# Four block boundaries of a one-core decoder kernel: which queue issues which load and store, and when

## The reference, cut to what matters

```python
x = x + tanh(g_xattn[0]) * L0_xattn(layernorm(x), ctx, ctx)      # 8 heads of 8, softmax over 256
x = x + tanh(g_ffn[0])   * L0_ffn(layernorm(x), ...)
x = x + tanh(g_xattn[1]) * L1_xattn(layernorm(x), ctx, ctx)      # q and k scaled to length 1 in each head
...
def L0_ffn(x, router_weight, router_bias, gate_up_proj, gate_up_bias, down_proj, down_bias):
    logits = x @ router_weight.T + router_bias                    # 16 experts
    top_val, top_idx = top_k(logits, 4); top_val = softmax(top_val)
    gate_up = einsum('th,ehd->etd', x, gate_up_proj) + gate_up_bias[:, None]   # 256 -> 512
    gate, up = min(gate_up[..., ::2], 7), clip(gate_up[..., 1::2], -7, 7)
    out = einsum('etd,edh->eth', (up + 1) * gate * sigmoid(1.702 * gate), down_proj) + down_bias[:, None]
    return sum over the token's 4 experts of score * out
```

## Time and profile before

| | |
|---|---|
| time, median of 3 runs | 3649.17 us (3646.26 to 3651.99) |
| the profiled execution: time / span of its instructions | 3641.4 us / 3639.7 us |
| PE busy / weight loads (PEld) | 2865.4 us (79%) / 1830.7 us (50%) |
| DVE / ACT / POOL busy | 2155.6 us (59%) / 1480.0 us (41%) / 1110.8 us (31%) |
| DMA | 386.10 MB, mean 106 GB/s |
| mean granted TensorE clock | 0.887 of 2.4 GHz |
| stretches, from the timeline: front; attention 0 | 0 to 144; 144 to 573 us |
| norms, router and ranks; scatter beside keys and values | 575 to 690; 691 to 926 us |
| experts 0; combine and split; attention 1 begins | 926 to 1421; 1426 to 1574; 1578 us |

### The profile page before, as it was taken

The page is one execution under the profiler, slowest core; times in us unless marked ns, Lnnn a source line. Parts: engine busy times, 40 slices in busy tenths (PEclk is TensorE's granted clock), DMA queues, the critical chain, the costliest instruction groups (busy, mean ns, idle before and its releaser), DMA issues. The chain is left out here.

```text
span 3639.7 us, 60306 instructions
## 1 busy us (share of the span) xinstructions
PE 2865.4 (79%) x20178; PEld 1830.7 (50%) x20178; DVE 2155.6 (59%) x4946; ACT 1480.0 (41%) x3032; POOL 1110.8 (31%) x1494
## 2 busy tenths in 40 slices
PE   5488884466699995579947798999989749999993
PEld 4233333222355553433323486454568638888782
DVE  7699993577577776634468687888868620000003
ACT  5377772155222223579935454222245211112120
POOL 3211110277233335512279542000034441111110
PEclk7599996599899998579968899999989669999996
DMA  7766643299422224858500341000044221112204
GB/s 255 204 117 119 119 103 139 91 366 363 166 81 81 79 82 123 201 97 118 101 1 1 123 150 56 1 1 1 1 141 143 92 63 57 50 54 65 72 28 139
DMA packets 261609, 386.10 MB, mean 106 GB/s; under 512 B 56865, under 2 KB 188942, under 8 KB 261056
## 3 DMA queue, kind: packets, MB, share of 16 engines
q1 hardware_dynamic: 236160, 314.07, 32.3%
q0 software_dynamic: 25152, 68.22, 5.4%
HBM read 227.49 MB, written 160.24 MB: 107 GB/s over the span
## 5 line engine op out<-in xcount | busy, mean ns | idle before, releaser
L3167 POOL DMA_INDIRECT rows_out<-e_out,e_tr_dest x224 | 235.5, 1051 | 870.8 <-DVE e_out L3804 504.4
L3804 DVE COPY e_out<-e_psD 128x512 f32<-128x512 f32 x40 | 27.7, 692 | 492.3 <-PE e_psD L3772 492.1
L1237 ACT ACTIVATE a_pt<-a_psS 128x512 f32<-128x512 f32 x512 | 277.6, 594 | 102.0 <-PE a_psS L1133 97.7
L1259 DVE TENSOR_REDUCE a_mx_sb<-a_psM 128x4 f32<-128x1024 f32 x256 | 293.2, 1213 | 9.2 <-PE a_psM L1116 8.2
L3572 PE MATMUL e_psG<-e_wgu,e_yT 128*128 x576 | 275.1, 600 | 25.9 <-ACT e_yT L3600 23.3
L1147 PE MATMUL a_psV<-a_pt,a_vt 128*18 128x256 f32 x4096 | 291.1, 386 | 1.2 <-issue 0.8
L3772 PE MATMUL e_psD<-e_w,e_hT 128*128 128x256 f32 x1280 | 289.9, 386 | 0.0
L3761 PE MATMUL e_psH<-e_yT,e_w 128*128 128x256 f32 x1280 | 284.9, 381 | 1.6 <-issue 0.8
L3704 ACT ACTIVATE e_hT<-e_psH 128x512 f32<-128x512 f32 x160 | 95.6, 597 | 452.6 <-PE e_psH L3761 452.6
L3761 PEld LDWEIGHTS e_psH<-e_yT,e_w 128*128 128x128 f32 x1280 | 244.4, 191 | 35.7 <-issue 2.1
L3772 PEld LDWEIGHTS e_psD<-e_w,e_hT 128*128 128x128 f32 x1280 | 245.5, 194 | 33.3
(11 more groups left out here) (433 smaller groups left out, 6221.1 us busy)
## 6 DMA issues: line engine op xcount, KB each, us to landing
kbd<-e_bgu SPq DMA_DIRECT2D x64, 512.0 KB, 4.6
cr_kbd<-kbd SPq DMA_DIRECT2D x64, 512.0 KB, 3.4
rows_in<-zeros POOLq DMA_DIRECT2D x36, 522.0 KB, 6.3
e_xin<-rows_in SPq DMA_DIRECT2D x144, 128.0 KB
vbd<-e_bd SPq DMA_DIRECT2D x64, 272.0 KB, 4.0
cr_vbd<-vbd SPq DMA_DIRECT2D x64, 272.0 KB, 2.6
cq_rows<-rows_out SPq DMA_DIRECT2D x32, 512.0 KB, 12.1
e_w<-in_L_ffn_w_dram SPq DMA_DIRECT2D x16, 1024.0 KB, 7.6
```

The costliest lines, as they stand in the source:

```text
L1237: act.activation(pt[:, probs(t, h), b, :, :], psS[:, unit(t, h, b) % S_BANKS, :].rearrange("p (k c) -> p k c", k=KC), ACT.Exp, scale=scale ...
L1259: dve.tensor_reduce(mx[:, t % 2, :, h, :], psM[:, k % 2, :, :].rearrange("p b (f c) -> p b f c", f=2), AX_X, ALU.max).then_inc(ring_read, 1)
L3167: pool.indirect_dma_start(out=self.rows_out[0:limit, :], out_offset=bass.IndirectOffsetOnAxis(ap=self.dest[:, t:t + 1], axis=0), in_=rows, ...
```

## The change

1. Front: slot 0 is loaded one group earlier (SP, end of group 2). SP keeps only the third piece's store of the last group; ACT issues the other two and the four `turned` stores at the end of its list. Slot 1 is loaded by SP at the start of the attention (`early` is 1, two slots stay allocated), followed by the values of tiles 0 and 1, the first shift, the next values and slot 2.
2. Layer 0's experts (`class Experts0`): the first matrices and their bias (`load_up`, 17 DMAs) are issued in `phase_project` behind the router's rows and bias. The second matrices (4 DMAs of 1024 KB) and their bias are issued by ACT in `phase_experts0` (`load_down`), behind its first copy of turned rows. `KeysValues` uses the room of the second matrices and second bias instead. PE waits for the second matrices before the first L3589, DVE for the bias before the first L3648. SP fetches the rows of tiles 0 and 1 ahead of the destinations.
3. Combine: slots 0 and 1 are loaded in steps 6 and 7, q and k together; slots 2 and 3 at the start of layer 1's attention.

```diff
@@ phase_front, sync @@
-                    if g == NG - 1:
+                    if g < NG - 1:
+                        for piece, n_done in enumerate((n_hi, n_mid, n_lo)):
+                            sp.wait_ge(n_done, g + 1)
+                            store_normal(sp, g, piece)
+                    if g == NG - 2:
                         for operand in ("q", "k"):
                             slots.load(sp, operand, 0)
-                    for piece, n_done in ((0, n_hi), (1, n_mid), (2, n_lo)):
-                        sp.wait_ge(n_done, g + 1)
-                        sp.dma_start(n_pieces[...], np[:, piece, :, :] ...).then_inc(n_stored, 16)
-                for m, (_, dst) in enumerate(pairs):
-                    sp.wait_ge(w_copied, m + 1)
-                    sp.dma_start(dst..., wt[:, m, :, :]).then_inc(w_stored, 16)
-                for operand in ("q", "k"):
-                    slots.load(sp, operand, 1)
+                sp.wait_ge(n_lo, NG)
+                store_normal(sp, NG - 1, 2)
                 sp.wait_ge(ct_stored, 16 * NG)
@@ phase_front, scalar @@
                 normal_mid(NG - 1)
+                act.wait_ge(n_hi, NG)
+                store_normal(act, NG - 1, 0)
+                act.wait_ge(n_mid, NG)
+                store_normal(act, NG - 1, 1)
+                act.wait_ge(w_copied, n_w)
+                for m, (_, dst) in enumerate(pairs):
+                    act.dma_start(dst..., wt[:, m, :, :]).then_inc(w_stored, 16)
@@ phase_attend, sync @@
+                for s in range(slots.early, 2):
+                    slots.load(sp, "q", s)
+                    slots.load(sp, "k", s)
                 load_values(0)
-                load_values(1)
-                if slots.early < BUFS:
-                    slots.load(sp, "q", 2)
                 if with_max:
                     shift(0)
-                if slots.early < BUFS:
+                load_values(1)
+                slots.load(sp, "q", 2)
+                if with_max:
                     sp.wait_ge(ones_set, 1)
-                    slots.load(sp, "k", 2)
+                slots.load(sp, "k", 2)
@@ phase_project, sync (phase_norms has no prefetch any more) @@
                     sp.dma_start(b[:, :], bias...).then_inc(bias_loaded, 16)
+                if prefetch is not None:
+                    prefetch(sp)
@@ phase_scatter, sync @@
                     pairs.sync(sp)
-                    late(sp)
@@ phase_combine_split, sync @@
-                    if i < slots.early:
-                        slots.load(sp, "k", i)
-                    if i in (4, 5):
-                        sp.wait_ge(stored[i % 2], 16 * PIECES)
-                        for s in range(2 * i - 8, 2 * i - 6):
-                            slots.load(sp, "q", s)
+                    if i == 4:
+                        sp.wait_ge(stored[0], 16 * PIECES)
+                    if 0 <= i - 6 < slots.early:
+                        slots.load(sp, "q", i - 6)
+                        slots.load(sp, "k", i - 6)
@@ expert_weights0 and expert_biases0 become class Experts0 @@
+    def load_up(self, sp):
+        for e in range(self.E):
+            sp.dma_start(self.wgu[:, e, :, :], self.gate_up[e]...).then_inc(self.up_loaded, 16)
+        sp.dma_start(self.bgu[:, :, :], self.gate_up_b...broadcast_to([P, self.E, self.D2])).then_inc(self.up_loaded, 16)
+
+    def load_down(self, eng):
+        n = self.E // self.PARTS
+        for m in range(self.PARTS):
+            eng.dma_start(self.wd[:, m * n:(m + 1) * n, :, :],
+                          self.down[m * n:(m + 1) * n]...).then_inc(self.down_loaded, 16)
+        eng.dma_start(self.bd[:, :, :], self.down_b...broadcast_to([P, self.E, self.D])).then_inc(self.bias_loaded, 16)
@@ phase_experts0 @@
+                    sp.dma_start(xin[:, t % 2, :], rows_in[t, :, 0:DIM]).then_inc(fetched[t % 2], 16)
+                    if t == 1:
+                        token_rows.load(sp, rows_in, 0)
+                    if t >= 1:
                         token_rows.load(sp, rows_in, t)
...
-                pe.wait_ge(loaded, 16 * (2 * E + 2))
+                pe.wait_ge(weights.up_loaded, 16 * (E + 1))
...
                         pe.wait_ge(h_copied, t + 1)
+                        if t == 0:
+                            pe.wait_ge(weights.down_loaded, 16 * weights.PARTS)
...
                     t, u = s + 2, s % 2
+                    if t == 1:
+                        weights.load_down(act)
...
                         dve.wait_ge(down_done, t + 1)
+                        if t == 0:
+                            dve.wait_ge(weights.bias_loaded, 16)
@@ flamingo_decoder @@
-            slots = Slots(core, c, "a0", q_pieces, k_pieces, 2)
+            slots = Slots(core, c, "a0", q_pieces, k_pieces, 1)
-            slots = Slots(core, held, "a1", q_pieces, n_pieces, Slots.BUFS)
+            slots = Slots(core, held, "a1", q_pieces, n_pieces, 2)
```

More of the change, by code:

```diff
@@ L174, in group, with store_normal @@
             return slice(g * G, (g + 1) * G)
+        def store_normal(eng, g, piece):
+            eng.dma_start(n_pieces[g, :, :, PIECES - 1 - piece].rearrange("b h d t c -> (b h) d (t c)"),
+                          np[:, piece, :, :].rearrange("p t c -> p (t c)")).then_inc(n_stored, 16)
         with nc.Block() as block:
@@ L250, in _ @@
                                    pattern=[[HD, H]], channel_multiplier=-1).then_inc(sel_made, 1)
-                for m in range(slots.early):
+                for m in range(slots.held_first):
                     pool.memset(slots.of("k", m), 1.0).then_inc(ones_set, 1)
@@ L442, in phase_norms @@
         with nc.Block() as block:
-            if prefetch is not None:
-                @block.sync
-                def _(sp):
-                    prefetch(sp)
             @block.vector
@@ L919, in __init__ @@
         self.loaded = [core.lasting_sem(f"{name}_ql{m}") for m in range(self.BUFS)]
-        self.hold(ctx, "first", range(early), "right")
+        self.hold(ctx, "first", range(held_first), "right")
     def hold(self, ctx, part, slots, side=None):
@@ L969, in phase_attend @@
         pt = core.sb(ctx, n + "_pt", [P, EXP_BUFS, 2, KC, DIM], F32)
[L970 to L971 removed]
+        slots.hold(ctx, "rest", range(slots.held_first, BUFS))
         ctl = core.sb(ctx, n + "_ctl", [P, 2, 2, 2 * KC, 2, 4, HD], F32)
@@ L1016, in _ @@
                 if with_max:
-                    for m in range(slots.early, BUFS):
+                    for m in range(2, BUFS):
                         pool.memset(slots.of("k", m), 1.0).then_inc(ones_set, 1)
@@ L2791, in _, with phase_scatter @@
                 c.link(dve.tensor_copy(slot[:, :, :], pos[:, :, :]))
-def phase_scatter(core, name, K, slot, rows_in, limit, mark, prefetch, pairs=None, late=None):
+def phase_scatter(core, name, K, slot, rows_in, limit, mark, prefetch, pairs=None):
     nc = core.nc
@@ L3616, in _ @@
                 expert = experts(mybir.EngineType.DVE)
-                dve.wait_ge(loaded, 16 * (2 * E + 2))
+                dve.wait_ge(weights.up_loaded, 16 * (E + 1))
                 for s in range(-1, T0 + 2):
```

83 lines of the change are left out of this document (39 added, 44 removed).

## The result

The changed kernel takes 3610.12 us (median, 3607.72 to 3616.43), the kernel before 3648.74 us on the same chip: a ratio of 0.9893, 95% interval 0.9879 to 0.9907, 38.6 us less. Run again later on another occasion it took 3614.80 us beside 3647.58 us, 0.9917 (0.9894 to 0.9941). The profiled execution of after has a span of 3607.1 us against 3639.7 us: 32.6 us less.

The account below looks back on a forecast made before the run. The prediction took DMA waits at four block boundaries, with no engine computing, as the bound. Front 8.2, router 15.3, experts 13.2 and combine 9.0 sum to 45.7 us: 3649.2 - 45.7 = 3603.5, range 3595 to 3618.

Parts of the forecast that it names:

- all four boundaries gain: Main case: front, router, experts and combine each get faster; 3603.5 us (3597 to 3611 by itself), chance 0.65.
- a new DMA wait of over 5 us: Sign that the prediction is wrong, if one of the four boundaries shows it in the changed profile.
- 12 take 6.0 to 8.7; I take 7.0: Front: us for SP to issue slot 0's 12 loads, by which PE's turning of the weights and all behind it move.
- I take the same 9.9 and allow 3 either way: Start of attention 0: us the first shift takes to land, unchanged although other loads now stand ahead of it.
- The second rival: Front: full DMA engines are the limit and all bytes remain, so the 8.2 us shrink to about 0; 3611.7, chance 0.11.
- Router: Router's start: norms no longer hold SP's loads, so the rows land earlier and PE starts 15.3 us earlier (14 to 16.5).
- Experts' start: Layer 0's experts: without the two late bias loads PE starts at 928.6, not 942.81, 14.2 us earlier.
- I take off 1.0: Experts: us lost to row fetches among the second weights' burst, leaving 13.2 us of gain (4 to 14.5).
- the first rival: Experts: the second weights become the wait and DVE's 11 us come off, less the 1.0 taken; 3613.5, chance 0.14.
- Combine: Combine and split: no attention loads in steps 0 to 5, 7.4 and 1.6 us, together 9.0 us gained (5 to 9.5).
- The third rival: Combine: q and k loads in steps 6 and 7 hold the stores, 1.6 to 7 of 9.0 us lost; 3608, chance 0.06.
- Slower by the clock: Experts: PE, starved after its earlier start, stays at a low clock; 3681 at 25 tiles, slower than before, chance 0.02.

Follow-up runs that it names:

- slot0_last: Changed kernel with slot 0's 12 loads issued behind the last group's k and q stores, not ahead of the context store and weight loads: 3609.65 us, ratio 0.9895.
- up_in_norms: Changed kernel with the first expert matrices and their bias (17 loads) issued in the norms again, ahead of the router's rows: 3625.52 us, ratio 0.9939.

## Why the prediction was right or wrong

The sign, the range (3595 to 3618) and two of the terms held: 3610.1, and 3614.8 in the later run. The value of 3603.5 was 6.6 us short, and what the forecast gave 0.65, "all four boundaries gain", was not what happened: two of the rivals were at work, each in part. That 3610.1 lies in the 3597 to 3611 of that case is no support for it: the rivals stood at 3608, 3611.7 and 3613.5, and the later 3614.8 lies outside. The prediction's own sign of being wrong came true at the front, "a new DMA wait of over 5 us" (5.99 us for the second shift), and DVE's wait of 2.66 us in the experts is over the 2 us that it allowed. One sum was off as well: the gains of the two weight and front rivals fall short by 10 and 8.2, which leaves 27.5 us and 3621.7, not the 3618 of the range.

*Front: the step "12 take 6.0 to 8.7; I take 7.0".* The issue time of the 12 loads was right (5.8 us); the delay of what is behind them was not. I counted SP's issuing and left out that the engines need longer for a slot than SP does. PE's weights came 12.5 us later, and ACT's stores took 6.8 us from its last piece, not 5.5. The end of the front moved by 3.05 us, 1.5 of them ahead of any edit. The step of the first shift, "I take the same 9.9 and allow 3 either way", erred the other way (5.3), which by luck put the first score near its forecast. The step behind it, that slot 2 and the second values come later and cost "nothing", failed as well: slot 2's loads and the shifts share the full engines, and the wait went from the first shift to the second. The second rival, DMA engines bound the front, is what holds in the main: it gave 0 for the part, the runs give 1.5 to 3.4 us. Its sign was another, though, the first score still near 167; it came at 159.87, and the gain was lost one shift later. It had the earlier trace rows for it, engines full at 220 GB/s, and the sum took nothing off for that. The rule of the Trainium skill beside it (DMA: Bandwidth & Descriptors, Issuing engines are not separate DMA queues: all issuing engines end on the same 16 DMA engines) agrees: in `slot0_last` the weights' turning came 11.7 us earlier, and tile 0's add 0.9 us (2.8 against the mean).

*Router: held.* 16.4 us for 15.3; the rows landed in 1.8 us, so the term was 1.2 short. `up_in_norms` shows the cause.

*Experts' start: held.* 14.25 us for 14.2, the last digits by luck.

*Second weights: the term "I take off 1.0" was mis-sized.* It measured 6.8 us. The time of the bytes was somewhat short (6.29 MB took 20.6 us, not 17.6, and the last landed 21.3 us behind PE's start; I had put it at 18.7). What the sum left out are the other users of the same engines: ACT's issues slowed to 9.1 us, beyond the 2.5 to 7 that I allowed, the row fetches came late, and a margin of 0.2 us for the bias was none. This is the first rival in part; it priced the burst at 10 us more than the forecast, the runs say 6.

*Combine: 7.4 of the 9.0.* The 1.6 us for the step of 11.59 us rested on a comparison with the step behind it. Both belong to the pipeline's end, and stay. The third rival, that the stores lose again to the new loads, is refuted: every step up to the sixth sum takes 14.3 us.

*Slower by the clock: refuted.* In the experts of after the granted clock is 1.00 (2.4 GHz) from 920 to 929 us, 12 us behind PE's start. It falls once more behind the row wait, to 0.64 from 929 to 933, and is 0.95 from 933 to 938: a tile's worth, not 25 tiles.

Against the forecast of 45.7 us: front -4.9, router +1.1, second weights -5.8, combine -1.6, and 1.2 in attention 0 that no term had: 35.8 us at attention 1's start, as the two timelines show (1577.96 - 1542.17).

## What to carry to other kernels

Before moving a load, read the DMA share and the GB/s of both the place it leaves and the place it goes to: where the share is near 1.0, moving issues between queues or up and down a list moves the wait and hardly the end, and low GB/s there is no room: here the slot loads filled the engines at 160 GB/s and the expert matrices at 348. Move the load to a stretch where the share is low, even at the cost of issues on the same queue. A margin computed from one transfer's landing time is no margin if small fetches of the running loop share the engines with a burst of megabytes.

## What the runs showed of the hardware

- Full engines can move very different amounts: 362 and 162 GB/s from 110 to 120 us, at shares of 1.04 and 1.00, without and with a slot's loads. Neither the number nor the size of the packets explains it: pieces of 1 KB passed at 348 GB/s elsewhere, and a burst of 6.29 MB took 20.6 us in 4304 packets and 21.7 us in 1231.
- A DMA issue's time depends on what is already in the engines: four loads of 1 MB and one of 2 MB took ACT 9.1 us; the same five with an eighth of the matrices' bytes and as many pieces 3.8 us; the 2 MB load by itself 3.10 us in the one and 0.60 us in the other.
- A fetch of 128 KB on SP's queue landed 19 us after its issue while 6.3 MB issued by POOL from 906.78 on, 2.3 us ahead of it, were moving. The Trainium skill (DMA: Bandwidth & Descriptors, Issuing engines are not separate DMA queues) says that DMAs of different engines interleave, and calls the issue time saved by a second engine "usually small relative to the DMA itself". Here the fetch came only with the end of the burst, so whatever interleaving there was did not help it; and ACT's 9.1 us beside a burst of 20.6 us were not small.
- In the last layer's experts the granted clock fell to 1.2 GHz for part of the next 11 us behind waits of PE of 3.81 and 2.66 us, and did not behind waits of 3.67 and 2.82 us at the same places in the other kernel: one fall cost 1.7 us.
